# Gather sums of a vision block: their products stream 96 columns instead of 8

## What is computed

```python
def _L0_ffn_ref(x, Wq_pk, pk_keys, Wq, keys_table, values_table, Wo):
    q = (x @ Wq).reshape(b, n, HEADS, DIM) * DIM ** (-0.5)
    kv_scores, indices = _pk(x, Wq_pk, pk_keys)        # 16 of 4096 rows for each token and head
    ind = indices + offsets[None, None, :, None]
    k = jnp.einsum('bnhk,bnhkd->bnhd', kv_scores, keys_table[ind])
    v = jnp.einsum('bnhk,bnhkd->bnhd', kv_scores, values_table[ind])
    sim = jnp.einsum('bihd,bjhd->bhij', q, k)
    ...
    return out @ Wo
```

## Time and profile before

| | us |
|---|---|
| median of 3 timed runs | 18092.87 |
| lowest, highest | 18075.98, 18133.94 |
| the profiled execution's own time | 18021.73 |
| its span in the trace | 18019.9 |
| mean granted TensorE clock over the span | 0.80 |

### The profile page before, as it was taken

How to read it: one execution, slowest core, us unless ns; L and a number is a source line. 1 busy time by engine, 2 the same in 40 slices (tenths; PEclk the granted TensorE clock), 3 DMA queues, 4 the chain that set the end, 5 groups by cost and what they waited for, 6 DMA issues and landing times.

```text
span 18019.9 us, 267276 instructions
## 1 busy us (share of the span) xinstructions
PE 14702.7 (82%) x73542; PEld 10792.0 (60%) x74812; DVE 10472.7 (58%) x39935; ACT 7685.2 (43%) x17286; POOL 10031.2 (56%) x9220
## 2 busy tenths in 40 slices
PE   5888888888888888888888888888888788888888
PEld 3655656656566665565665656665556566565566
DVE  6665656656556556555655655656655556556562
ACT  2444444444444444444444444444444444444443
POOL 2555555555555555555555555555555555555554
PEclk6888888878878778777878877888878788878887
DMA  2444444434434444334443443444434434444333
GB/s 78 115 119 107 114 113 111 114 108 114 114 104 116 111 109 116 104 112 110 112 113 105 116 117 104 115 114 110 115 104 114 114 106 113 109 113 115 105 111 89
DMA packets 1643062, 1984.59 MB, mean 110 GB/s; under 512 B 527806, under 2 KB 1129022, under 8 KB 1628990
## 3 DMA queue, kind: packets, MB, share of 16 engines
q1 hardware_dynamic: 1346366, 1359.69, 26.6%
q0 software_dynamic: 294912, 604.57, 13.1%
HBM read 1898.00 MB, written 65.01 MB: 109 GB/s over the span
## 4 chain that ended last, share of the span: by engine, by line
PE 45%; another core or an unknown queue 16%; issue 16%; DVE 14%; ACT 5%; DMA 2%; SPq 1%; DVEq 0%; ACTq 0%
PE bank L889 11%; PE bank L924 7%; PE bank L906 3%; PE bank L766 3%; PE bank L911 3%; PE bank L913 2%; PE bank L874 2%; PE bank L813 2%; DMA moving<-keyspace 2%; ACT over L1157 2%; PE bank L895 2%; DVE decay L1471 1%; PE bank L954 1%; DVE apart L1607 1%
## 5 line engine op out<-in xcount | busy, mean ns | idle before, releaser
L694 POOL DMA_INDIRECT gath<-in_table_dram,rowsT x9216 | 10031.0, 1088 | 7940.7 <-PE bank L924 4563.1
L889 PE MATMUL bank<-weight,rowtab 128*128 128x256 f32 x12288 | 4792.1, 479 | 918.1 <-issue 376.0
L1157 ACT ACTIVATE over<-bank,seventeen 128x512 bf16<-128x512 f32 x3584 | 2465.2, 688 | 3432.0 <-PE bank L906 1539.1
L1163 ACT ACTIVATE weight<-bank 128x512 f32<-128x512 f32 x3584 | 2135.1, 596 | 3871.8 <-remote 1777.0
L889 PEld LDWEIGHTS bank<-weight,rowtab 128*128 128x128 f32 x12288 | 2687.4, 239 | 1614.1 <-issue 1078.5
L924 PEld LDWEIGHTS bank<-spread,gath 128*128 128x128 f32 x18432 | 2898.3, 225 | 189.4 <-issue 1.1
L924 PE MATMUL bank<-spread,gath 128*128 128x8 f32 x18432 | 2608.8, 268 | 2.0 <-issue 1.7
L906 PE MATMUL bank<-moving,pick_b 96*128 96x512 bf16 x3584 | 1552.5, 433 | 278.0 <-issue 204.1
L1728 DVE TENSOR_REDUCE negmax<-bank 128x1 f32<-128x128 f32 x512 | 148.1, 289 | 2733.5 <-PE bank L955 1627.1
L911 PE MATMUL bank<-moving,pick_b 96*128 96x512 bf16 x3584 | 1654.3, 462 | 2.3 <-issue 2.3
L1739 DVE SCALAR_TENSOR_TENSOR acc<-bank,rrow,acc 128x64 f32<-128x64 f32 x1024 | 245.7, 279 | 2093.7 <-issue 1471.6
(11 more groups left out here) (267 smaller groups left out, 20850.8 us busy)
## 6 DMA issues: line engine op xcount, KB each, us to landing
rowtab<-in_tableD_dram SPq DMA_DIRECT2D x2048, 256.0 KB
wide<-states SPq DMA_DIRECT2D x512, 512.0 KB
moving<-keyspace SPq DMA_DIRECT2D x3072, 64.0 KB
gath<-in_table_dram,rowsT POOLq DMA_INDIRECT x9216
moving<-keyspace SPq DMA_DIRECT2D x3072, 32.0 KB
pix<-in_x_dram SPq DMA_DIRECT2D x64, 1024.0 KB
pix<-in_x_dram SPq DMA_DIRECT2D x128, 512.0 KB
keyspace<-split SPq DMA_DIRECT2D x192, 256.0 KB, 2.0
```

The source lines that it names most:

```text
L694: pool.indirect_dma_start(out=gath[:, u % RING, j, :], out_offset=None, in_=table, in_offset=bass.IndirectOffsetOnAxis(ap=rowsT[k][:, col: ...
L889: last = mm(dense_ps[:, 0:TOK], rowtab[:, r, s % 2 * 2 + half, :], weight[s % 2][:, half * TOK:(half + 1) * TOK], start=(s % 16 == 0 and h ...
L1157: af(over[:], d_ps[:], ACT.Relu, scale=-1.0, bias=seventeen[:, 0:1]).then_inc(over_ready, 1)
L1163: af(weight[s % 2][:], z_ps[:], ACT.Exp).then_inc(weight_ready, 1)
```

## The change

`STREAM` is 96. Each product of the gather sums streams 96 columns from `spread` and writes 96 columns of `sums_ps`, from the same first column as before. The first eight are the sums as before; the 88 others are products of this gather's rows with later gathers' weights, and are overwritten by the products that follow, each of which starts anew at its own column, or lie in columns beyond the 256 that are copied out. `spread` grows by 11 groups of 8 columns for each of the five heads' buffers, which are set to zero once, before the loop. The number of instructions in the loop and their order are the same on all engines.

```diff
+STREAM = 96
...
-        spread = [sb(f"spread{g}", [P, SPAN, 8]) for g in range(GH)]
+        spread = [sb(f"spread{g}", [P, SPAN + STREAM // 8 - 1, 8]) for g in range(GH)]
...
                 for j in range(PART):
                     col = (i * PART + j) * 8
-                    last = mm(sums_ps[:, col:col + 8], gath[:, u % RING, j, :],
-                              spread[ORDER[g]][:, i * PART + j, :], start=True, stop=True)
+                    flat = spread[ORDER[g]][:].rearrange("p i c -> p (i c)")
+                    last = mm(sums_ps[:, col:col + STREAM], gath[:, u % RING, j, :],
+                              flat[:, col:col + STREAM], start=True, stop=True)
                 last.then_inc(summed, 1)
...
+                for g in range(GH):
+                    step(v.memset(spread[g][:, SPAN:, :], 0.0))
...
-                v.tensor_tensor(spread[o][:], src, own[:].unsqueeze(1).to_broadcast([P, SPAN, 8]),
+                v.tensor_tensor(spread[o][:, 0:SPAN, :], src, own[:].unsqueeze(1).to_broadcast([P, SPAN, 8]),
                                 ALU.mult).then_inc(spread_ready, 1)
```

## The result

| | us |
|---|---|
| kernel before, median of 6 runs beside it | 18098.92 |
| changed kernel, median of 6 runs | 17929.99 |
| lowest, highest | 17883.06, 17995.33 |
| ratio, 95% interval | 0.9909, 0.9884 to 0.9934 |
| span of its profiled execution | 17923.4 |

The change gains 169 us, 0.9%, where 725 us, 4.0%, were forecast. The page of the changed kernel, the lines that answer to the earlier trace rows: busy times, granted clock in 40 slices, chain by engine.

A forecast was written before the change was run, and what follows sets the result against it. TensorE was taken as the bound, slowed by half clock. 2,280 us less at half, worth 0.38 each, gain 866 us; less 141 us for wider streams, net 725 us (4.0%), giving 17,360 us, range 16,850 to 18,000.

The forecast's parts named there:

- What bounds the kernel: TensorE, busy 82% of the span, at half clock about 7,100 us; thinly streaming gather bursts keep the clock low.
- The wider streams, 141 us: 2304 gather bursts on TensorE: 96 columns add 0.05 us each at full clock, 0.09 at half; bounds 0 and 213 us.
- The upper bound: All eight steps of a burst as long as with 128 columns: 0.07 us more at full, 0.15 at half.
- The guess at where the price lies: Within a burst, only the first matmul's step follows its columns; the other seven follow the weight loads.
- The amount of clock, 2,280 us: TensorE's half-clock time behind each stretch's first burst, at most 3,250 us: 70% goes, mean clock rises to 0.86.
- The worth of 1 us at half, 0.38: Each microsecond less at TensorE's half clock shortens the kernel by 0.38 us, a gain of 866 us before costs.
- The bounds of the forecast: Worth of 1 us at half: 0.50 if PE sets everything, 0.30 from comparing images of low and high clock.
- The rival that came true is the first: Clock rises but time is given back on waits; worth 0.1, about 18,000 us; chance 0.10.
- the exponentials' loop: PE and ScalarE's two exponentials in a slot wait for each other: 1539 and 1439 us of ScalarE waits for PE.
- if the clock is up and the span is not down (worth of the clock): Sign of failure for the whole kernel: it would show the assumed 0.38 us per microsecond at half wrong.
- the range: Kernel time expected between 16,850 and 18,000 us, leaving out about 0.2 of the chances.

The follow-up runs named there:

- the second pair: Kernel before and changed kernel timed again in a later session: 17736.68 us before, 17655.82 us changed, ratio 0.9955.
- one32: Kernel before with one product of 32 columns in a burst in place of four of 8: 17056.19 us, ratio 0.9625.
- fourth_twice8: Kernel before with each of the gather sums' products issued twice, 8 columns each: 18879.48 us, ratio 1.0640.
- gath1: Kernel before with one gather in a part in place of four, TensorE's instructions unchanged: 13899.61 us, ratio 0.7844.
- gath2: Kernel before with two gathers for each part in place of four: 13969.34 us, ratio 0.7891.

## Why the prediction was wrong, by its own steps

**What bounds the kernel: read half.** That the clock is low because bursts are holes in the streaming was right: the clock rose with the columns in every pair, and with PE's busy share it did not. What I passed over stood in the earlier trace rows as "another core or an unknown queue 16%". I took PE's 82% and 45% as the bound and gave that 16% no term. It was the sign of waits for 3,700 us of the kernel's time.

**The wider streams, 141 us: right.** A burst went from 0.81 to 0.86 us at full and from 1.57 to 1.65 at half, where 0.05 and 0.09 were forecast. The forecast took the share of time at full clock, 72%, for the share of bursts at full, which is 84%; with that it is 2304 x (0.84 x 0.054 + 0.16 x 0.086) = 136 us of TensorE's time. The upper bound, steps as long as with 128 columns, was not reached. The guess at where the price lies was right too: by the medians of both traces a burst's first step went from 0.028 to 0.082 us at full and from 0.072 to 0.160 at half, and the other seven stayed at 0.112 and 0.213.

**The amount of clock, 2,280 us: nearly right.** The time at half went from 7,196 to 5,228 us, 1,968 less, and the clock to 0.854 where 0.86 was forecast. The place is the forecast one: in 56 images the time at half behind the first burst of its stretch fell from 3,008 to 905 us, to 30%, where 70% was to go; ahead of the bursts it rose from 3,081 to 3,508, so that the sum is smaller.

**The worth of 1 us at half, 0.38: this step failed.** Measured are (169 + 136) / 1,968 = 0.15 at most, if the streams' price counts in full; by the second pair (81 + 135) / 1,522 = 0.14. The bounds of the forecast were 0.30 and 0.50, so the value lies below what I had called the lower bound. 0.50 assumed that TensorE's time counts in full, and `one32` and `fourth_twice8` show 0.37 and 0.50 for it. A microsecond at half costs half a microsecond of TensorE's work, so by these it could be worth 0.19 to 0.25. The 0.30 came from comparing images: those with less clock were longer. I read that as the clock's effect on the time. But `gath1` shows the reverse arrow, strong: waits gone, clock 0.811 to 0.928. An image that happens to hold more of these waits is longer by the waits and has a lower clock by the same waits. A comparison between images cannot tell the two, and it isn't a bound for what a change of the clock alone does.

**The rival that came true is the first,** time given back on waits, at 0.1 and some 18,000 us; I gave it 0.10. It was nearly right in the price and wrong in the place: not the exponentials' loop but waits that no recorded work ends. Of the forecast's own tests of failure, "if the clock is up and the span is not down (worth of the clock)" is nearly what happened. The measured time lies within the range, near its upper end.

**What stays open.** With 0.19 to 0.25 for a microsecond at half, and the streams at 0.37 to 0.50 of 136 us, the first pair should have gained some 310 to 420 us and the second 230 to 310; they gained 169 and 81. Of the way from the forecast's 0.38 to the measured 0.15, the last 0.04 to 0.10 is thus without a cause. In both pairs the standing still grew by some 400 us (1,241 to 1,645, and 1,082 to 1,463), about as much as by `one32` (428 us), which saved more than twice the TensorE time. Why the faster clock meets these waits so squarely the runs don't say. Nor do they say what delays the updates, nor why whole sessions are free of it. One rival stands untested. In the slow condition six of ten records of the DMAs' updates are missing (below), and each timed run here comes with a record of the clock; that the waits come from the recording of so many updates, and not from the gathers as such, is not ruled out.

## What to carry to other kernels

Before a faster engine is priced, find what its microsecond is worth: take a known piece of its work out, or put it in twice. Here these would have said 0.4 and 0.5, and the forecast of 4% would have been one of 2 to 3%, still above the 0.9% that came. Don't take such a worth from a correlation inside one trace, where a common cause moves both sides; and give every share of the chain its own line in the sum, the one called unknown above all.

## What the runs showed of the hardware

- The granted clock answers to the columns streamed, not to PE's busy share: 8, 48, 96, 128 and 224 columns in the same products give 0.926, 0.933, 0.943, 0.953 and 0.967 in the quick condition (PE 89% busy, 93% with 224), and 0.80 to 0.81 goes to 0.854 and 0.857 in the slow one; twice as many products of 8 columns give 0.877 and 0.872 with PE 94 and 95% busy. The Trainium skill ("TensorE: Matmul & The Clock Gate", section "What's actually happening") has the gate follow how busy the PE has recently been. Read as the busy share of the profile, these runs speak against it.
- Each of the two matmuls of a float product whose weights are new each time takes a step of 0.112 us at full and 0.213 at half (medians), with 8 columns and with 96; only the first step of a burst follows the columns, 0.028 us with 8, 0.082 with 96 and 0.109 with 128 at full. A burst of eight matmuls takes 0.81 us with 8 columns at full, 0.86 with 96 and 0.89 with 128; with 224 columns a step takes 0.189 us.
- In the slow condition this kernel's 9,216 indirect gathers go with 3,700 to 3,800 us of waits, whether they bring 605 or 303 MB; with 4,608 or 2,304 gathers these waits are gone. The two that were looked at are semaphore updates of work that had ended some 7 us earlier, as far as the trace tells. The records suffer too: the trace of before holds 119,646 updates by DMAs in the slow condition and 301,164 in the quick one, for the same DMAs. That alone doesn't make a kernel slow: `gath2`, quick in a slow session, holds 156,260, where 227,436 would be left if each gather left out took its 16 updates with it.
- The same kernel on the same chip took 14,061 us in one session and 17,712 in another. Two kernels are to be compared side by side in one session, and a gain is to be given with the condition in which it was measured: this change is worth 0.5 to 0.9% in the slow one and 0.7% in the quick one, and 1.5% once three of four gathers are gone.
